# Edge stage 1 of a two-layer graph network: the gathered rows of c are added by the DMA onto a pre-activation that ACT has copied

## The chip, the cores and the metric

One Trainium2 chip, one core. The metric is the device time of one execution in microseconds (us). Lower is better. PE is TensorE, DVE is VectorE, ACT is ScalarE, POOL is GpSimd, SP is SyncE. SP and POOL issue the DMAs: SP the plain ones, POOL the indirect ones (gathers).

## The reference, cut to what matters

12,500 nodes with 128 features, 200,000 edges sorted by `dst`, 64 edge features. Layer 0 is an attention-like graph layer with a residual and a layer norm. Layer 1 is:

```python
src, dst = edge_indices[0], edge_indices[1]
edge_inputs = concatenate([x[src], x[dst], edge_features], axis=1)
h = edge_inputs @ W1 + b1
h = (h - mean(h)) * rsqrt(var(h) + 1e-5) * ln_g + ln_b
h = relu(h)
messages = (h @ W2 + b2) * sigmoid(edge_features @ gate_w + gate_b)
agg = segment_sum(messages, dst, num_segments=12500)
# then a GRU cell on (agg, x), a residual and a layer norm
```

Everything per edge up to the segment sum is edge stage 1. The part of `h` that comes from one end of the edge is made per node before the stage and is a table in HBM, `c` (12,500 rows of 128 floats). The part of the other end is a table in SBUF, `near`, one tile of 128 nodes after another. W2 is applied after the sum. W1 is centred beforehand, so the mean of `h` is zero and the layer norm needs only the sum of squares.

## The kernel before, in words

The program runs as stages one after the other: constants, a sort of the edges on DVE, a schedule, layer 0, edge stage 1 (`edge_stage1`, from line 1440), the GRU stage.

Edge stage 1 works on 1664 steps of 128 edges, in 208 groups of G = 8. Every engine has its own program over the same step numbers, made by `loop_groups`: step 0 to 207, and some steps more at the end, so that an engine can work on a group some steps after it was begun. In the text "step g" of an engine is the body of `steps(g, ...)` on that engine, and "group g-2" is the group worked on there under `has(g, 2)`. An engine's queue is in order: its step g+1 begins when its step g is issued. The engines meet by semaphores alone. R = 4 is the number of gather buffers (`crows`), edge feature buffers (`ef`) and index buffers (`cols`). The other buffers are in pairs.

One step of each engine before the change:

- SP (line 1526 on) loads the edge features, the row of node places (`spread`), and, once `hotw` and the gather of the group four before are done, the indices (`cols`) of a group.
- POOL (line 1566 on) waits for the indices and for `pre_used` of the group that had the buffer before, and issues 8 indirect DMAs (line 1559), each of 128 rows of `c` into `crows`. So it can run up to four groups ahead of DVE.
- PE, step g: turns the edge features of group g (line 1587) into `efT_ps`; makes the pre-activation `pre` of group g-1 from the turned features and from `near` by a one-hot matrix (lines 1600 and 1602), half by half; then scatters group g-3 (line 1615), for which it needs `hotw` and `z` of group g-3.
- ACT, step g: copies `efT` of group g (line 1635), makes `hotT` of group g (1641, 1645); then, when DVE has made `h` of group g-1, the exponential `eg` of the gate (1653), eight squares with their sums (1660), logarithm and exponential for the norm (`rstd`, 1666 and 1672), all of group g-1.
- DVE, step g: `h` of group g-1 = `pre` + `crows` in two halves (1703, which counts `pre_used`); then, when `rstd` of group g-2 is there, `z` of group g-2 (1712, 1728) in turns with adding the scattered sums of group g-3 (1722); `hotw` of group g-2 (1733); then the gate of group g-1 from `eg` (1743, 1745).

`h` has 129 columns: 128 for the norm, the last for the gate. `pre` fills four PSUM banks and has one buffer.

Of the kernel before, what the change touches and what calls it, by code (L numbers as in the profile page):

```python
# [20 lines left out]
ACT = mybir.ActivationFunctionType  # L21
F32 = mybir.dt.float32
# [4 lines left out]
P = 128  # L27
N = 12500
E = 200000
D = 128  # L30
# [6 lines left out]
G = 8  # L37
# [1402 lines left out]
def edge_stage1(nc, s, ins):  # L1440

    W = D + 1
    with ExitStack() as ctx:
# [14 lines left out]
        h = [sb(f"h1_{i}", [P, G, W], F32) for i in range(2)]  # L1458
# [14 lines left out]
        ef_in = [sem(f"ef_in{q}") for q in range(R)]  # L1473
        hotT_made, ef_turned, efT_made = sem("hotT1_made"), sem("ef_turned"), sem("efT_made")
        pre_made, pre_used, gate_read = sem("pre1_made"), sem("pre1_used"), sem("gate_read")
# [9 lines left out]
        with nc.Block() as block:  # L1485
# [63 lines left out]
            @block.gpsimd  # L1549
            def _(pool):  # L1550
                pool.wait_ge(zeroed, 1)
                for i in range(2):
                    nc.gpsimd.memset(z[i][:, :, D:W], 1.0).then_inc(zeroed, 1)
                for q in range(R):
                    nc.gpsimd.memset(crows[q][:, :, D:W], 0.0).then_inc(zeroed, 1)

                def gather(q):
                    for k in range(G):
                        pool.indirect_dma_start(  # L1559
                            out=crows[q][:, k, 0:D], out_offset=None, in_=s.c[:, :],  # L1560
                            in_offset=bass.IndirectOffsetOnAxis(ap=cols[q][:, 0, k:k + 1], axis=0),
                        ).then_inc(rows_in[q], 16)
                for q in range(R):
                    pool.wait_ge(cols_in[q], 16)
                    gather(q)
                with pool.Fori(1, BODIES) as o:
                    for q in range(R):
                        pool.wait_ge(cols_in[q], o * 16 + 16)

                        pool.wait_ge(pre_used, (o - 1) * (2 * R) + 2 * q + 2)  # L1570
                        pool.sem_inc(issue, 1)
                        gather(q)

            @block.tensor
            def _(pe):
                pe.wait_ge(steps_in, 32)
                pe.wait_ge(w_in, 16 * 7)
                pe.wait_ge(zeroed, R + 3)
                pe.wait_ge(added, 1)

                def steps(g, q, o):
# [9 lines left out]
                    if has(g, 1):  # L1591
# [4 lines left out]
                        for half in range(2):  # L1596
                            if used(g, 2):
                                pe.wait_ge(pre_used, g * 2 + half - 3)
# [23 lines left out]
            def _(act):  # L1622
# [4 lines left out]
                def steps(g, q, o):  # L1627
                    par, other = q % 2, 1 - q % 2
                    if has(g, 0):
                        act.wait_ge(ef_turned, g + 1)  # L1630
                        if used(g, 2):

                            act.wait_ge(pre_used, g * 2 - 2)
# [13 lines left out]
                    if has(g, 1):  # L1647
                        act.wait_ge(pre_used, g * 2)
                        if used(g, 3):
                            act.wait_ge(eg1_made, g - 2)  # L1650
                        act.sem_inc(act_go, 1)

                        nc.scalar.activation(eg[:, other, :], h[other][:, :, D], ACT.Exp,  # L1653
                                             bias=gb[:, 0:1], scale=-1.0).then_inc(gate_read, 1)
                        for half in range(2):
                            if used(g, 2) or half:
                                act.wait_ge(ss_made, g * 2 - 2 + half)
                            act.sem_inc(act_go, 1)
                            for k in range(4 * half, 4 * half + 4):
                                last = nc.scalar.activation(sq[:, k % 4, :], h[other][:, k, 0:D], ACT.Square,  # L1660
                                                            accum_out=ss[:, other, k:k + 1])
                            last.then_inc(ss_made, 1)
                        act.wait_ge(ss_made, g * 2)
# [4 lines left out]
                        act.wait_ge(ln_made, g)  # L1668
                        if used(g, 3):
                            act.wait_ge(scaled, g * 2 - 4)  # L1670
# [3 lines left out]
                loop_groups(act, steps, 1)  # L1674

            @block.vector
            def _(dve):
# [8 lines left out]
                dve.wait_ge(zeroed, R + 3)  # L1686
# [3 lines left out]
                def steps(g, q, o):  # L1690
                    par, other = q % 2, 1 - q % 2
                    if has(g, 1):
                        p1 = (q - 1) % R
                        dve.wait_ge(rows_in[p1], o * (16 * G) + (0 if q == 0 else 16 * G))
                        if used(g, 3):
# [380 lines left out]
```

## Time and profile before

| | us |
|---|---|
| median of 3 runs | 5315.48 (5291.51 to 5352.39) |
| the profiled execution's own time | 5289.88 |
| its span in the profile | 5288.0 |
| busy: PE, DVE, ACT, POOL | 3398.4, 4096.3, 2249.5, 3334.9 |

The span is what the profile sees from the first to the last instruction. Busy times are unions over the whole span, so they average over stages with different limits. Edge stage 1 is the stretch from about 2760 to 4957 us.

### The profile page before, as it was taken

How to read it: one execution, taken by the hardware profiler on the slowest of the kernel's cores; microseconds unless marked ns; L12 is line 12 of the kernel's file. 1: busy time of each engine (PE TensorE's matmuls, PEld its weight loads, DVE VectorE, ACT ScalarE, POOL GpSimd, SP SyncE). 2: the span in 40 equal slices, each digit the busy share in tenths (PEclk: the TensorE clock that was granted, in tenths of full speed). 3: DMA queues.
4: the chain of work that ended last, by engine and by line, in shares of the span. 5: the costliest groups of instructions: out<-in, count | busy, mean ns of one | idle time of the engine just before them, and what ended most of it. 6: DMA issues, size and time to landing. Idle time of an engine off the chain costs nothing. (4 is left out here: it accounts for less than half of the span.)

```text
span 5288.0 us, 106563 instructions
## 1 busy us (share of the span) xinstructions
PE 3398.4 (64%) x20476; PEld 3032.9 (57%) x20477; DVE 4096.3 (77%) x15676; ACT 2249.5 (43%) x6299; POOL 3334.9 (63%) x3474
## 2 busy tenths in 40 slices
PE   5511366666666666666647776677776776667797
PEld 4411255555555555555546765666666666667564
DVE  8998567777777777777767888888888888888655
ACT  1210123333333333333326555555555555555323
POOL 0000577777777777777757777777777777777210
PEclk9755567777777877778768889988889889998898
DMA  4100344545555555545534444444444344444102
GB/s 127 53 0 9 114 130 139 144 142 142 143 143 142 141 144 144 142 142 143 144 95 106 102 103 103 101 102 102 101 101 101 99 102 101 103 103 102 41 22 61
DMA packets 626386, 565.35 MB, mean 107 GB/s; under 512 B 376509, under 2 KB 491880, under 8 KB 625924
## 3 DMA queue, kind: packets, MB, share of 16 engines
q0 software_dynamic: 133952, 329.07, 23.0%
q1 hardware_dynamic: 492356, 235.40, 16.9%
q8 instruction: 28, 0.46, 0.0%
q14 instruction: 50, 0.41, 0.0%
HBM read 531.83 MB, written 38.57 MB: 108 GB/s over the span
## 5 line engine op out<-in xcount | busy, mean ns | idle before, releaser
L1559 POOL DMA_INDIRECT crows<-c,cols x1664 | 1659.3, 997 | 511.0 <-issue 474.9
L1115 POOL DMA_INDIRECT bxrows<-bx,cols x1664 | 1611.6, 968 | 510.0 <-issue 506.9
L1160 PE MATMUL scattered<-bxrows,hotw 128*128 128x129 f32 x3328 | 703.5, 382 | 631.3 <-DVE hotw L1321 630.8
L1160 PEld LDWEIGHTS scattered<-bxrows,hotw 128*128 128x128 f32 x3328 | 613.8, 276 | 709.8 <-DVE acc L1318 628.3
L1615 PE MATMUL scattered<-z,hotw 128*128 128x129 f32 x3328 | 585.8, 346 | 547.5 <-DVE hotw L1733 547.4
L1615 PEld LDWEIGHTS scattered<-z,hotw 128*128 128x128 f32 x3328 | 536.8, 248 | 586.3 <-issue 568.6
L1600 PE MATMUL pre<-w1e,efT 128*128 128x129 f32 x3328 | 686.5, 289 | 100.4 <-DVE h L1703 92.4
L1318 DVE TENSOR_TENSOR acc<-acc,scattered 128x129 f32 x1664 | 475.4, 286 | 326.7 <-ACT mask L1231 323.7
L1712 DVE SCALAR_TENSOR_TENSOR z<-h,rstd,ln_g 128x128 f32<-128x128 f32 x1664 | 579.5, 349 | 157.6 <-issue 157.5
L1602 PE MATMUL pre<-near,hotT 128*128 x3328 | 661.9, 282 | 0.0
L1150 PE MATMUL pre<-near,hotT 128*128 x3328 | 560.6, 338 | 147.8 <-DVE h L1297 115.8
L1150 PEld LDWEIGHTS pre<-near,hotT 128*128 128x128 f32 x3328 | 527.1, 248 | 195.9 <-issue 191.5
L1600 PEld LDWEIGHTS pre<-w1e,efT 128*128 128x128 f32 x3328 | 534.2, 202 | 134.0 <-DVE h L1703 121.1
L1321 DVE SCALAR_TENSOR_TENSOR hotw<-lane,cols,mask 128x128 f32<-128x128 f32 x1664 | 578.6, 348 | 2.3 <-ACT mask L1231 2.2
L1602 PEld LDWEIGHTS pre<-near,hotT 128*128 128x128 f32 x3328 | 528.4, 200 | 0.0
L1660 ACT ACTIVATE sq<-h 128x128 bf16<-128x128 f32 x1664 | 490.5, 296 | 25.5
L1722 DVE TENSOR_TENSOR acc<-acc,scattered 128x129 f32 x1664 | 472.5, 284 | 2.3 <-PE scattered L1615 1.0
L1224 ACT ACTIVATE sig<-logit,b 128x8 f32<-128x8 f32 x208 | 62.6, 301 | 960.5 <-DVE h L1304 960.0
L1733 DVE SCALAR_TENSOR_TENSOR hotw<-lane,cols,gate 128x128 f32<-128x128 f32 x1664 | 454.7, 347 | 0.0
L1703 DVE TENSOR_TENSOR h<-pre,crows 128x516 f32<-128x516 f32 x416 | 270.2, 691 | 199.6 <-DMA crows<-c,cols 173.3
L1653 ACT ACTIVATE eg<-h,neg_gate_b 128x8 f32<-128x8 f32 x208 | 63.9, 307 | 756.6 <-DVE h L1703 751.2
L1297 DVE TENSOR_TENSOR h<-pre,bxrows 128x512 f32<-128x512 f32 x416 | 268.2, 687 | 145.4 <-DMA bxrows<-bx,cols 135.8
(262 smaller groups left out, 5430.5 us busy)
## 6 DMA issues: line engine op xcount, KB each, us to landing
spread<-place_rows SPq DMA_DIRECT2D x416, 256.0 KB
ef<-in_edge_attr SPq DMA_DIRECT2D x1664, 32.0 KB
bxrows<-bx,cols POOLq DMA_INDIRECT x1664
crows<-c,cols POOLq DMA_INDIRECT x1664
cols<-columns SPq DMA_DIRECT2D x416, 8.0 KB, 1.9
bx<-in_x SPq DMA_DIRECT2D x1, 6250.0 KB
x_a<-in_x SPq DMA_DIRECT2D x97, 64.0 KB
x_b<-in_x SPq DMA_DIRECT2D x97, 64.0 KB
```

Of the source, the lines that this page charges most:

```text
L1115: pool.indirect_dma_start(out=bx[q][:, k, 0:2 * D], out_offset=None, in_=s.bx[:, :], in_offset=bass.IndirectOffsetOnAxis(ap=cols[q][:, 0, ...
L1150: last = nc.tensor.matmul(pre[:, k, :], hotT[par][:, k * P:(k + 1) * P], s.near[:, bass.ds(tiles[k], 1), :], start=True, stop=True)
L1160: last = nc.tensor.matmul(out[:, k // 2, k % 2, 0:W], hotw[v % 2][:, k, :], bx[v][:, k, D:D + W], start=True, stop=True)
L1318: dve.tensor_tensor(there, there, out[:, k // 2, k % 2:k % 2 + 1, 0:W], ALU.add).then_inc(added, 1)
L1321: last = dve.scalar_tensor_tensor(hotw[other][:, k, :], s.lane[:, :], cols[v].bitcast(F32)[:, 1, k:k + 1], mask[:, other, k:k + 1].to_broa ...
L1559: pool.indirect_dma_start(out=crows[q][:, k, 0:D], out_offset=None, in_=s.c[:, :], in_offset=bass.IndirectOffsetOnAxis(ap=cols[q][:, 0, k: ...
L1600: nc.tensor.matmul(pre[:, k // 2, k % 2, 0:W], efT[par][:, k // 2, :], w1e2[:, k % 2, :], start=True, stop=False)
L1602: last = nc.tensor.matmul(pre[:, k // 2, k % 2, 0:D], hotT[par][:, k * P:(k + 1) * P], s.near[:, bass.ds(tiles[k], 1), :], start=False, st ...
L1615: last = nc.tensor.matmul(out[:, bank, at:at + W], hotw[par][:, k, :], z[par][:, k, :], start=True, stop=True)
L1660: last = nc.scalar.activation(sq[:, k % 4, :], h[other][:, k, 0:D], ACT.Square, accum_out=ss[:, other, k:k + 1])
L1712: last = dve.scalar_tensor_tensor(z[par][:, k, 0:D], h[par][:, k, 0:D], rstd[:, par, k:k + 1], ln_g[:, :], ALU.mult, ALU.mult)
L1722: dve.tensor_tensor(place, place, out[:, bank:bank + 1, at:at + W], ALU.add).then_inc(added, 1)
```

## The change

ACT copies `pre` with its 129 columns from PSUM into the gather's buffer `crows`, in two halves, at its step g for group g-1. It counts them in `h_copied`. The gather of a group waits for that copy, and its DMA adds the rows of `c` onto the 128 columns that it writes (`compute_op=ALU.add`). So `crows` then holds `h`, and the addition on DVE and the buffers `h` are gone. ACT's statistics (gate exponential, squares, `rstd`) wait for the gather and move from group g-1 to group g-3 of ACT's step g. ACT's loop gets three further steps at the end in place of one. PE's next `pre` waits for `h_copied` in place of `pre_used`. DVE's parts keep their steps: `z` and `hotw` of group g-2, sums of group g-3, gate of group g-1. `z` now waits also for the scatter of group g-4. Of the edge stage nothing else changes.

```diff
-        h = [sb(f"h1_{i}", [P, G, W], F32) for i in range(2)]
@@ POOL
-                for q in range(R):
-                    nc.gpsimd.memset(crows[q][:, :, D:W], 0.0).then_inc(zeroed, 1)
                 def gather(q):
                     for k in range(G):
                         pool.indirect_dma_start(
                             out=crows[q][:, k, 0:D], out_offset=None, in_=s.c[:, :],
                             in_offset=bass.IndirectOffsetOnAxis(ap=cols[q][:, 0, k:k + 1], axis=0),
+                            compute_op=ALU.add,
                         ).then_inc(rows_in[q], 16)
                 for q in range(R):
                     pool.wait_ge(cols_in[q], 16)
+                    pool.wait_ge(h_copied, 2 * q + 2)
+                    pool.sem_inc(issue, 1)
                     gather(q)
...
-                        pool.wait_ge(pre_used, (o - 1) * (2 * R) + 2 * q + 2)
+                        pool.wait_ge(h_copied, o * (2 * R) + 2 * q + 2)
@@ PE
-                                pe.wait_ge(pre_used, g * 2 + half - 3)
+                                pe.wait_ge(h_copied, g * 2 + half - 3)
@@ ACT
-                            act.wait_ge(pre_used, g * 2 - 2)
+                            act.wait_ge(pre_made, g * 2 - 2)
...
                     if has(g, 1):
-                        act.wait_ge(pre_used, g * 2)
-                        if used(g, 3):
-                            act.wait_ge(eg1_made, g - 2)
+                        v = (q - 1) % R
+                        if used(g, 5):
+                            act.wait_ge(scaled, g * 2 - 8)
+                        for half in range(2):
+                            act.wait_ge(pre_made, g * 2 - 1 + half)
+                            act.sem_inc(act_go, 1)
+                            cut = slice(4 * half, 4 * half + 4)
+                            nc.scalar.copy(crows[v][:, cut, :],
+                                           pre.rearrange("p b t d -> p (b t) d")[:, cut, 0:W]).then_inc(h_copied, 1)
+                    if has(g, 3):
+                        v = (q - 3) % R
+                        other = (q - 3) % 2
+                        act.wait_ge(rows_in[v], (o + (0 if q < 3 else 1)) * (16 * G))
+                        if used(g, 3 + 2):
+                            act.wait_ge(eg1_made, g - 3 - 1)
                         act.sem_inc(act_go, 1)
-                        nc.scalar.activation(eg[:, other, :], h[other][:, :, D], ACT.Exp,
+                        nc.scalar.activation(eg[:, other, :], crows[v][:, :, D], ACT.Exp,
...
-                loop_groups(act, steps, 1)
+                loop_groups(act, steps, 3)
@@ DVE
-                    if has(g, 1):
-                        p1 = (q - 1) % R
-                        dve.wait_ge(rows_in[p1], o * (16 * G) + (0 if q == 0 else 16 * G))
-                        if used(g, 3):
-
-                            dve.wait_ge(scaled, g * 2 - 4)
-                            dve.wait_ge(ss_made, g * 2 - 4)
-                            dve.wait_ge(gate_read, g - 2)
-                        for half in range(2):
-                            dve.wait_ge(pre_made, g * 2 + half - 1)
-                            cut = slice(4 * half, 4 * half + 4)
-                            dve.tensor_tensor(h[other][:, cut, :],
-                                              pre.rearrange("p b t d -> p (b t) d")[:, cut, 0:W],
-                                              crows[p1][:, cut, :], ALU.add).then_inc(pre_used, 1)
...
                     if has(g, 2):
+                        v = (q - 2) % R
                         dve.wait_ge(rstd_made, g - 1)
+                        if used(g, 4):
+                            dve.wait_ge(scattered, g * 3 - 9)
                     for k in range(G):
                         if has(g, 2):
-                            last = dve.scalar_tensor_tensor(z[par][:, k, 0:D], h[par][:, k, 0:D],
+                            last = dve.scalar_tensor_tensor(z[par][:, k, 0:D], crows[v][:, k, 0:D],
```

## Rows read from the trace of the kernel before

**Rows 1.** Page, groups of POOL, DVE and ACT in the edge stage.

```profile
L1559 POOL DMA_INDIRECT crows<-c,cols x1664 | 1659.3, 997 | 511.0 <-issue 474.9
...
L1703 DVE TENSOR_TENSOR h<-pre,crows 128x516 f32<-128x516 f32 x416 | 270.2, 691 | 199.6 <-DMA crows<-c,cols 173.3
```

**Rows 2.** Stretches: start, length, busy (xcount) of PE, PEld, DVE, ACT, POOL, PEclk, DMA.

```profile
2777.00:4957.00 2180.00, 1524.18 (x10816) 1450.95 (x10816) 1816.86 (x6240) 1258.36 (x4576) 1646.08 (x1655) 0.88 0.41 100
```

**Rows 3.** Timeline of DVE, one step, 3503 to 3513 us.

```profile
3503.82 1.30 DVE L1703 TENSOR_TENSOR h<-pre,crows 128x516 f32<-128x516 f32 x2 [1.04 <-DMA crows<-c,cols]
3505.85 0.35 DVE L1712 SCALAR_TENSOR_TENSOR z<-h,rstd,ln_g 128x128 f32<-128x128 f32 x1 [0.73 <-issue]
...
3510.80 2.18 DVE L1733 SCALAR_TENSOR_TENSOR hotw<-lane,cols,gate 128x128 f32<-128x128 f32 x8
```

**Rows 4.** Timeline of ACT, 3505 to 3512.3 us.

```profile
3505.27 0.31 ACT L1653 ACTIVATE eg<-h,neg_gate_b 128x8 f32<-128x8 f32 x1 [3.88 <-DVE h L1703]
...
3508.76 0.21 ACT L1672 ACTIVATE rstd<-lnv 128x8 f32<-128x8 f32 x1 [0.20 <-ACT lnv L1666]
3509.33 0.59 ACT L1635 COPY efT<-efT_ps 128x512 f32<-128x512 f32 x1 [0.36 <-issue]
...
3511.09 1.15 ACT L1645 ACTIVATE hotT<-off,one 128x1024 f32<-128x1024 f32 x1
```

**Rows 5.** Timeline of PE at full clock, 3512 to 3519.4 us.

```profile
3512.07 2.12 PE L1615 MATMUL scattered<-z,hotw 128*128 128x129 f32 x16 [2.71 <-DVE hotw L1733]
3514.03 0.60 PE L1587 MATMUL efT_ps<-ident_f,ef 128*128 128x128 f32 x4
3515.56 0.48 PE L1600 MATMUL pre<-w1e,efT 128*128 128x129 f32 x2 [0.92 <-DVE h L1703]
...
3519.01 0.39 PE L1602 MATMUL pre<-near,hotT 128*128 x2
```

**Rows 6.** Timeline of PE, the next burst, begun at half clock.

```profile
3522.65 3.80 PE L1615 MATMUL scattered<-z,hotw 128*128 128x129 f32 x16 [3.26 <-DVE hotw L1733]
3526.25 1.06 PE L1587 MATMUL efT_ps<-ident_f,ef 128*128 128x128 f32 x4
3527.10 0.64 PE L1600 MATMUL pre<-w1e,efT 128*128 128x129 f32 x2
...
3528.38 0.39 PE L1602 MATMUL pre<-near,hotT 128*128 x2
...
3531.06 0.39 PE L1602 MATMUL pre<-near,hotT 128*128 x2
```

**Rows 7.** Stretches of 1 us around it; the fourth number is the granted clock.

```profile
3523.00:3524.00 1.00, 1.00 (x6) 0.50 0.26 72
...
3529.00:3530.00 1.00, 1.00 (x11) 1.00 0.52 120
```

**Rows 8.** Timeline of DVE, hotw of the step after that of rows 3.

```profile
3521.38 2.18 DVE L1733 SCALAR_TENSOR_TENSOR hotw<-lane,cols,gate 128x128 f32<-128x128 f32 x8
```

**Rows 9.** Timelines at the stage's start: first gather, first z, second h.

```profile
2761.03 0.95 POOL L1559 DMA_INDIRECT crows<-c,cols  x1 [1.25 <-DMA cols<-columns]
...
2791.91 0.70 DVE L1703 TENSOR_TENSOR h<-pre,crows 128x516 f32<-128x516 f32 x1 [2.03 <-PE pre L1602]
...
2796.53 1.13 DVE L1712 SCALAR_TENSOR_TENSOR z<-h,rstd,ln_g 128x128 f32<-128x128 f32 x4
```

**Rows 10.** Timelines at the stage's end: last gather, last h, last group's z.

```profile
4929.12 0.95 POOL L1559 DMA_INDIRECT crows<-c,cols  x1 [0.30 <-issue]
...
4933.95 1.30 DVE L1703 TENSOR_TENSOR h<-pre,crows 128x516 f32<-128x516 f32 x2 [2.83 <-DMA crows<-c,cols]
...
4945.02 0.35 DVE L1712 SCALAR_TENSOR_TENSOR z<-h,rstd,ln_g 128x128 f32<-128x128 f32 x1 [1.69 <-issue]
```

**Rows 11.** DMA queues from 3000 to 5000 us: packets, MB, share of 16 engines.

```profile
q0 software_dynamic: 47489, 97.35, 19.6%
```

**Rows 12.** Timeline of POOL, two gathers of one group.

```profile
3532.81 1.53 POOL L1559 DMA_INDIRECT crows<-c,cols  x1 [0.31 <-issue]
3534.65 0.95 POOL L1559 DMA_INDIRECT crows<-c,cols  x1 [0.30 <-issue]
```

More of the change, by code:

```diff
@@ L1473, in edge_stage1 @@
         ef_in = [sem(f"ef_in{q}") for q in range(R)]
+        h_copied, z_scaled_up = sem("h_copied"), sem("z_scaled_up")
         hotT_made, ef_turned, efT_made = sem("hotT1_made"), sem("ef_turned"), sem("efT_made")
-        pre_made, pre_used, gate_read = sem("pre1_made"), sem("pre1_used"), sem("gate_read")
+        pre_made, gate_read = sem("pre1_made"), sem("gate_read")
         ss_made, ln_made, rstd_made = sem("ss_made"), sem("ln_made"), sem("rstd1_made")
@@ L1577, in _ @@
                 pe.wait_ge(w_in, 16 * 7)
-                pe.wait_ge(zeroed, R + 3)
+                pe.wait_ge(zeroed, 3)
                 pe.wait_ge(added, 1)
@@ L1647, in steps @@
                     if has(g, 1):
-                        act.wait_ge(pre_used, g * 2)
-                        if used(g, 3):
-                            act.wait_ge(eg1_made, g - 2)
+                        v = (q - 1) % R
[13 more added lines that the diff above has]
+                            act.wait_ge(eg1_made, g - 3 - 1)
                         act.sem_inc(act_go, 1)
-                        nc.scalar.activation(eg[:, other, :], h[other][:, :, D], ACT.Exp,
+                        nc.scalar.activation(eg[:, other, :], crows[v][:, :, D], ACT.Exp,
                                              bias=gb[:, 0:1], scale=-1.0).then_inc(gate_read, 1)
                         for half in range(2):
-                            if used(g, 2) or half:
-                                act.wait_ge(ss_made, g * 2 - 2 + half)
+                            if used(g, 3 + 1) or half:
+                                act.wait_ge(ss_made, (g - 3) * 2 + half)
                             act.sem_inc(act_go, 1)
                             for k in range(4 * half, 4 * half + 4):
-                                last = nc.scalar.activation(sq[:, k % 4, :], h[other][:, k, 0:D], ACT.Square,
+                                last = nc.scalar.activation(sq[:, k % 4, :], crows[v][:, k, 0:D], ACT.Square,
                                                             accum_out=ss[:, other, k:k + 1])
                             last.then_inc(ss_made, 1)
-                        act.wait_ge(ss_made, g * 2)
+                        act.wait_ge(ss_made, (g - 3) * 2 + 2)
                         act.sem_inc(act_go, 1)
@@ L1667, in steps @@
                                              scale=1.0 / D).then_inc(ln_made, 1)
-                        act.wait_ge(ln_made, g)
-                        if used(g, 3):
-                            act.wait_ge(scaled, g * 2 - 4)
+                        act.wait_ge(ln_made, g - 3 + 1)
+                        if used(g, 3 + 2):
+                            act.wait_ge(scaled, (g - 3) * 2 - 2)
                         act.sem_inc(act_go, 1)
@@ L1685, in _ @@
                 dve.wait_ge(negated, 2)
-                dve.wait_ge(zeroed, R + 3)
+                dve.wait_ge(zeroed, 3)
                 spread_b = neg_b[:, :].rearrange("p (a d) -> p a d", a=1).to_broadcast([P, 4, D])
@@ L1691, in steps @@
                     par, other = q % 2, 1 - q % 2
-                    if has(g, 1):
-                        p1 = (q - 1) % R
-                        dve.wait_ge(rows_in[p1], o * (16 * G) + (0 if q == 0 else 16 * G))
-                        if used(g, 3):
-                            dve.wait_ge(scaled, g * 2 - 4)
-                            dve.wait_ge(ss_made, g * 2 - 4)
-                            dve.wait_ge(gate_read, g - 2)
-                        for half in range(2):
-                            dve.wait_ge(pre_made, g * 2 + half - 1)
-                            cut = slice(4 * half, 4 * half + 4)
-                            dve.tensor_tensor(h[other][:, cut, :],
-                                              pre.rearrange("p b t d -> p (b t) d")[:, cut, 0:W],
-                                              crows[p1][:, cut, :], ALU.add).then_inc(pre_used, 1)
                     if has(g, 3):
```

## The prediction

> **What bounds the kernel now.** I read the page's costliest groups first, then the stretch of the stage, then the timelines of the four engines over one step, since a step repeats 208 times. In the group of the gathers [rows 1] the reader is to see that POOL's busy time and its idle time, 1659.3 + 511.0, fill the stage, and that nearly all the idle time (474.9) is "issue": POOL waits for nobody. 1664 gathers from 2761.03 to 4930.07 [rows 9, 10] are 1.30 us each, 10.4 us for the 8 of a group. DVE's addition in the same rows shows the other side: it stood 173.3 us waiting for the gather's data, 0.83 us per group. DVE was busy 1816.86 of 2180 us, ACT 1258.36 and PE 1524.18 [rows 2], so each has room in a period of 10.4 us. The stage goes at POOL's pace. From the first z at 2796.53 to that of the last group at 4945.02 [rows 9, 10] there are 207 periods, 2148.5 / 207 = 10.38 us each.
>
> **What the order of the steps allows.** Before, the statistics of a group are made one ACT step earlier than the z that needs them asks for: ACT makes rstd of group g-1 in its step g, DVE uses it in its step g+1. That slack lets ACT, DVE and PE work side by side. The change moves ACT's statistics back by two groups (to g-3 in step g) and leaves z at group g-2 of DVE's step g. So DVE's step g now needs ACT's step g+1, a step ahead of it. Follow what ACT's step g+1 needs before it reaches the statistics of group g-2:
>
> - PE's turn of the features of group g+1, and both halves of `pre` of group g, for the new copies. These are PE's step g+1.
> - PE's step g+1 is queued behind its step g, whose last part is the scatter of group g-3. It waits for `hotw` of group g-3, which DVE makes near the end of its step g-1.
>
> So a ring closes over one step: end of hotw in DVE's step g-1, scatter, turn, pre (PE), copy and statistics (ACT), z to hotw in DVE's step g. Nothing in it overlaps with anything else in it, apart from what is counted below. The gate (1743, 1745) needs `eg` of ACT's step g+2 at the end of DVE's step g, which lies on the same ring, 3.4 us before rstd, and costs nothing more. The length of this ring is the period, if it is above 10.4 us.
>
> **The ring's length, step by step.**
>
> - DVE from z to the end of hotw: 3505.85 to 3510.80 + 2.18 = 3512.98, 7.13 us [rows 3].
> - PE begins the scatter 0.91 us before that end, as the first half of hotw is enough: 3512.07 against 3512.98 [rows 3, 5], and likewise 3522.65 against 3521.38 + 2.18 = 3523.56 [rows 6, 8].
> - PE's burst scatter, turn, pre. The clock decides here. At full clock the scatter begins at 3512.07, the turn ends at 3514.63, and pre takes 3515.56 to 3519.40, 3.84 us [rows 5]. In [rows 5] pre still waited for DVE's h. After the change it follows the turn at once (its wait is for a copy one period old), begins at 14.5 and ends at 18.4. In [rows 6] the burst begins after 3.26 us of idle time at the half clock (0.50, 1.2 GHz), and is unbroken: scatter 3.80, turn until 3527.31, pre from 3527.10, the spacing falls from 0.43 to 0.22 us at 3528.38, the end is 3531.45. [Rows 7] show the granted clock at 0.50 in 3523 to 3524 and 1.00 from 3529.
> - ACT: the turned features are copied 0.15 us after the turn ends (that is the lag between DVE's h ending at 3505.12 and eg starting at 3505.27 [rows 3, 4]). From the efT copy to the end of hotT it is 3509.33 to 3512.24, 2.91 us. Then the copies of pre. The trace has no copy of 128x516 out of PSUM on ACT. The nearest is efT, 128x512 PSUM to SBUF, 0.59 us [rows 4]. I take 0.59 for each half. It can't be much below, and twice that, 1.2 us, is my upper bound (DVE's add of the same shape, with a second input, takes 0.69 [rows 1]); at that bound the ring is 0.6 us longer, +125 us in all, inside the range. The second half counts after pre ends: lag 0.15 + 0.59.
> - Statistics, from eg to the end of rstd: 3505.27 to 3508.97, 3.70 us [rows 4]. Then 0.15 us to z. The 0.73 us "issue" ahead of z in [rows 3] is register loading of tile numbers, and now lies beside the ring, between gate and rstd.
>
> With the full clock throughout, from z at 3505.85: pre ends 3518.40, second copy 3519.14, rstd 3522.84, z 3522.99. ACT's own path is shorter (14.63 + 0.15 + 2.91 = 17.69, then the first copy until 18.28). Ring 17.1 us.
>
> With the burst as in [rows 6]: hotw ends 3523.56, pre ends 3531.45, second copy 3532.19, rstd 3535.89, z 3536.04: 12.48 us after hotw's end, plus 7.13 = 19.6 us. With the half clock throughout the spacing would stay at 0.43 after 3528.38: 12 spacings by 0.21 and a longer last matmul, 2.8 us later [rows 6]. Ring 22.4 us.
>
> After the change PE is idle between pre and the next scatter for 19.6 - 8.8 = 10.8 us, three times the 3.26 us after which it began at the half clock in [rows 6]. So every burst begins slow. Its length unbroken is that of [rows 6], so I take it as it stands: 19.5 us, a little below 19.6 as ACT's second copy may begin without the full lag.
>
> **What lies beside the ring.** DVE loses the addition, 1.30 us per group [rows 3]. Before, it ran while POOL set the pace, and after, it isn't on the ring: it gives nothing. ACT gains 1.2 us per group: counted. POOL issues the same 8 DMAs, 10.4 us per group. It now starts a group when both copies of it are made, and ACT needs the data two ACT steps later, about 39 us minus the statistics. So 10.4 us of issue and 3.9 us of landing (last gather 4930.07 to last h 4933.95 [rows 10]) are covered with a margin of more than 20 us, and POOL's pace hides under 19.5 us as long as a gather takes less than 19.5 / 8 = 2.4 us against 1.30. SP's queue: indices of a group wait for hotw and gather of the group four before, and the features of the next group stand behind them. That wait ends with DVE's step g-2, a whole period before PE's step g+1 needs the features; before it was the same, with a shorter period. The memsets of crows on POOL and the third and fourth waits (`scaled`, `scattered`) are for things long done: nothing.
>
> **The gather with an addition** isn't in the trace. From below, its issue costs what the plain one costs, 0.95 us and 0.30 us between two [rows 12]; nothing that it leaves out would make it cheaper. From above I have only far rows: the longest plain one in the step of [rows 12] took 1.53 us, in place of the 0.95 of its neighbour. The transfer: 47489 packets took 19.6% of 16 engines over 2000 us [rows 11], 0.13 us each, 32 packets to one gather of 1484, 2 for each DMA engine. Reading the destination as well makes this perhaps 0.5 to 0.8 us for each engine per gather, against 2.4 us. I take it as hidden. If it isn't, the stage follows it (a rival below).
>
> The Trainium skill's page "DMA: Bandwidth & Descriptors", section "Rules for kernel authors", says that an accumulating DMA reads its destination and writes it later. That speaks against the change: each row is read twice and written once. It gives no price, no row here shows one, and by my bound it stays below the ring.
>
> **The sum.** The first z now needs the first gather, which before ran beside everything from 2761. Second half of pre at 2791.9 [rows 9], copy until 2792.5, 8 gathers at 1.25 [rows 12] = 10.0 us, landing 3.9, statistics 3.7, z at about 2810.2: 13.7 us later than 2796.5. Then 207 periods of 19.5 us = 4036.5 in place of 2148.5: +1888. The last two rings have no turn and no pre, about 6 us less each: -12. Together +1890. 5288.0 + 1890 = 7178 span, and with the 1.9 us around it 7180 us. The profiled execution (5289.88) lies 0.5% below the median of the runs, 5315.48, and inside their range. A measurement of this kernel tells about 1% from no change; this is 36%.
>
> **Rivals.**
>
> 1. *The clock takes another course, ring as said.* Full clock always (17.1 us): 5290 + 207 x 6.7 + 2 = 6680. Half clock always (22.4): 7780. For the first speaks nothing, with 10 us of idle time; for the second that the trace has few bursts after so long a gap. These are the bounds of my own case.
> 2. *The gather with an addition becomes the bound.* At 3.0 us each, 24 us per group: 5290 + 207 x 13.6 + 2 = 8110, and growing with its price, from 2.4 us on. For it: POOL is the bound now, and the operation is unknown. Against: it would have to cost nearly twice the plain one.
> 3. *Not slower.* The ring doesn't bind, because PE's pre of group g runs beside or ahead of the scatter's wait for hotw, and POOL stays the bound. It decides below 10.4 us of ring. Then DVE's shed 1.30 us gives nothing, but POOL's gathers could fall to 0.95 + 0.30 = 1.25 us each (8 x 1.25 = 10.0): 5290 - 207 x 0.38 + 14 = 5225. Against it: every engine takes its queue in order, and in [rows 5] the scatter stood 2.71 us waiting for hotw with the turn of the next group behind it.
> 4. *The addition doesn't run as one DMA* but in pieces with their own waits, so that the landing passes 39 us and holds up ACT. It ends slower too, above 8100. A part of case 2 for the numbers.
>
> **How the numbers follow.** Ring as forecast, with its clock bounds: 0.81 (own range 6680 to 7780). Gather-bound, cases 2 and 4: 0.13. Not slower: 0.04, half of it within 1% and half faster by over 1%. Slower by some other, smaller amount (a shorter ring of 11 to 16 us because I missed an overlap): 0.02. The range 6680 to 7800 leaves out the gather-bound case, the not slower one, and a little at each end. Chances: faster by over 1% 0.02; within 1% 0.02; slower by over 1% 0.81 + 0.13 + 0.02 = 0.96.
>
> **What the profile after would show.** If right: z (DVE) starts every 19 to 20 us; between the gate and z DVE stands 7 to 8 us waiting, put down to ACT's rstd or eg; ACT waits for pre of PE ahead of its copies; PE stands some 10 us ahead of the scatter waiting for hotw, and its granted clock over the stage falls from 0.88 to 0.6 to 0.8; POOL, idle about 9 us per group, waits for ACT's copy. Wrong, if POOL's gathers stand back to back (case 2 with a longer mean, case 3 with the old one), if ACT's wait ahead of eg is for the DMA, or if the period is below 16 us.

## The result and the profile after

The changed kernel took 7034.48 us (median of 4 runs, 7020.41 to 7085.32), the kernel before beside it 5303.49 us. Ratio 1.326, 95% interval 1.3145 to 1.3374. The profiled execution has a span of 7019.3 us against 5288.0, 1731 us more.

Five of the page's costliest groups after. Columns: line, engine, operation, tiles, shapes and count; busy us, mean ns of one; idle us of the engine just before them, and what ended most of it.

```profile
L1557 POOL DMA_INDIRECT crows<-c,cols x1664 | 2722.0, 1636 | 1191.0 <-ACT crows L1656 745.9
...
L1616 PE MATMUL scattered<-z,hotw 128*128 128x129 f32 x3328 | 757.4, 418 | 2213.5 <-DVE hotw L1735 2213.5
...
L1745 DVE TENSOR_SCALAR eg<-eg 128x8 f32<-128x8 f32 x208 | 35.7, 172 | 1719.3 <-ACT eg L1666 1719.3
L1714 DVE SCALAR_TENSOR_TENSOR z<-crows,rstd,ln_g 128x128 f32<-128x128 f32 x1664 | 574.4, 345 | 629.6 <-ACT rstd L1685 627.6
L1636 ACT COPY efT<-efT_ps 128x512 f32<-128x512 f32 x208 | 121.9, 586 | 2235.8 <-PE efT_ps L1588 2235.8
```

Read these as a circle. ACT stands 2235.8 us waiting for PE's turn (line 1588, the edge features turned into `efT_ps`), PE 2213.5 for DVE's hotw, DVE 1719.3 + 627.6 for ACT's eg and rstd. Each waits some 11 us in each of 208 steps for the engine before it, and none is the bound by its own work. POOL, which before waited for hardly anyone (36.1 of its 511.0 us idle weren't issue), waits 745.9 us for ACT's copies. So the gathers aren't the bound either, although one now takes 1.64 us in place of 1.00.

The stretch of the stage after, columns as in [rows 2]:

```profile
2900.00:6600.00 3700.00, 1588.31 (x10244) 1540.29 (x10244) 1476.19 (x5516) 1379.68 (x4728) 2580.72 (x1577) 0.68 0.36 56
```

PE is busy 43% of it, DVE 40%, ACT 37%. Before it was 70, 83 and 58% [rows 2]. The granted clock's mean fell from 0.88 to 0.68.

The period is best read from one line: the first and the last start of DVE's hotw, between which lie 207 periods and 1.9 us inside a group. For line 1735 the view of one source line (duration in ns min/median/max, first and last start) has:

```profile
L1735 DVE SCALAR_TENSOR_TENSOR hotw<-lane,cols,gate x1664: 336/343/371, 2812.6 to 6683.3; 128x128 f32<-128x128 f32 x185
```

and the same line of the kernel before:

```profile
L1733 DVE SCALAR_TENSOR_TENSOR hotw<-lane,cols,gate x1664: 337/348/384, 2800.1 to 4952.2; 128x128 f32<-128x128 f32 x185
```

(3870.7 - 1.9) / 207 = 18.69 us per group against (2152.1 - 1.9) / 207 = 10.39. The first hotw came 12.5 us later. 12.5 + (3870.7 - 2152.1) = 1731.1 us, the whole difference of the spans. Nothing is left over for another stage.

18.69 is a mean over all periods, and the last two are shorter. From DVE's timeline (start, length):

```profile
6662.76 2.18 DVE L1735 SCALAR_TENSOR_TENSOR hotw<-lane,cols,gate 128x128 f32<-128x128 f32 x8
...
6672.27 2.18 DVE L1735 SCALAR_TENSOR_TENSOR hotw<-lane,cols,gate 128x128 f32<-128x128 f32 x8
...
6681.51 2.18 DVE L1735 SCALAR_TENSOR_TENSOR hotw<-lane,cols,gate 128x128 f32<-128x128 f32 x8
```

They take 9.5 and 9.2 us. The 205 ahead of them, from 2812.61 to 6662.76, are 18.78 us each.

One turn of the ring after, in the order in which the work goes. DVE's timeline:

```profile
4805.23 2.18 DVE L1735 SCALAR_TENSOR_TENSOR hotw<-lane,cols,gate 128x128 f32<-128x128 f32 x8
4814.97 0.17 DVE L1745 TENSOR_SCALAR eg<-eg 128x8 f32<-128x8 f32 x1 [7.56 <-ACT eg L1666]
...
4818.38 0.35 DVE L1714 SCALAR_TENSOR_TENSOR z<-crows,rstd,ln_g 128x128 f32<-128x128 f32 x1 [3.00 <-ACT rstd L1685]
...
4823.32 2.18 DVE L1735 SCALAR_TENSOR_TENSOR hotw<-lane,cols,gate 128x128 f32<-128x128 f32 x8
```

PE's timeline, two bursts:

```profile
4806.50 3.40 PE L1616 MATMUL scattered<-z,hotw 128*128 128x129 f32 x16 [10.73 <-DVE hotw L1735]
4809.74 0.60 PE L1588 MATMUL efT_ps<-ident_f,ef 128*128 128x128 f32 x4
...
4813.55 0.39 PE L1603 MATMUL pre<-near,hotT 128*128 x2
4824.59 3.80 PE L1616 MATMUL scattered<-z,hotw 128*128 128x129 f32 x16 [10.66 <-DVE hotw L1735]
4828.18 1.06 PE L1588 MATMUL efT_ps<-ident_f,ef 128*128 128x128 f32 x4
...
4832.77 0.39 PE L1603 MATMUL pre<-near,hotT 128*128 x2
```

ACT's timeline, the first turn and the copies of the second:

```profile
4810.54 0.59 ACT L1636 COPY efT<-efT_ps 128x512 f32<-128x512 f32 x1 [10.38 <-PE efT_ps L1588]
...
4812.30 1.15 ACT L1646 ACTIVATE hotT<-off,one 128x1024 f32<-128x1024 f32 x1
4813.35 1.29 ACT L1656 COPY crows<-pre 128x516 f32<-128x516 f32 x2
4814.54 0.31 ACT L1666 ACTIVATE eg<-crows,neg_gate_b 128x8 f32<-128x8 f32 x1
...
4818.03 0.21 ACT L1685 ACTIVATE rstd<-lnv 128x8 f32<-128x8 f32 x1 [0.20 <-ACT lnv L1679]
...
4832.26 0.57 ACT L1656 COPY crows<-pre 128x516 f32<-128x516 f32 x1
4833.28 0.59 ACT L1656 COPY crows<-pre 128x516 f32<-128x516 f32 x1 [0.46 <-PE pre L1603]
```

hotw ends at 4807.41. PE has begun 0.91 us earlier, turns until 4810.34, ends pre at 4813.94. ACT takes the turned features 0.20 us after, copies pre until 4814.64, has rstd at 4818.24, and z starts at 4818.38. hotw ends at 4825.50, 18.1 us after the last. That is the first of the two rings shown. In the second PE's burst (scatter, turn and pre, one after the other) takes 8.57 us in place of 7.44, since its clock rises later. Stretches of 1 us, columns as in [rows 2], the granted clock third from the end:

```profile
4809.00:4810.00 1.00, 1.00 (x10) 1.00 (x9) 0.00 (x0) 0.00 (x0) 0.86 (x1) 0.83 0.45 56
...
4828.00:4829.00 1.00, 1.00 (x6) 1.00 (x6) 0.00 (x0) 0.00 (x0) 0.78 (x1) 0.50 0.20 22
4829.00:4830.00 1.00, 1.00 (x8) 1.00 (x7) 0.00 (x0) 0.56 (x2) 0.92 (x1) 0.59 0.56 71
```

The first burst began at 4806.50, and in the stretch from 4809 its clock is at 0.83; the second began at 4824.59 and is still at 0.50 from 4828 and at 0.59 from 4829. The second ring is 19.2 us. In both, and in every one of the 205, ACT's second copy begins 0.12 us after pre ends: it is PE's burst that ACT waits for there.

The mean of each part over the 205 rings adds up to the period: burst 8.09, less the 0.91 that lie before hotw's end; 0.12 to the second copy; 0.49 from it to eg; statistics 3.71; 0.17 to z; z to the end of hotw 7.11. Together 18.78.

POOL's timeline in the same turn:

```profile
4810.99 1.55 POOL L1557 DMA_INDIRECT crows<-c,cols  x1 [0.30 <-issue]
4815.43 1.55 POOL L1557 DMA_INDIRECT crows<-c,cols  x1 [2.89 <-ACT crows L1656]
```

The last gather of a group ends at 4812.54, POOL waits for the copy and goes on at 4815.43, 2.89 us later. Per group its slack is 18.7 less 8 x 1.94, 3.2 us in the mean.

### The profile page after: what moved, and what is told of

It is laid out like the page before. It is cut to its first block and busy times, and to the rows that moved or that the text cites. A ratio compares the mean times of both kernels' runs of the same rounds, so it can differ in the third digit from the quotient of the medians.

```text
span 7019.3 us, 107281 instructions
## 1 busy us (share of the span) xinstructions
PE 3555.0 (51%) x20476; PEld 3209.9 (46%) x20477; DVE 3837.5 (55%) x15260; ACT 2448.3 (35%) x6715; POOL 4396.3 (63%) x3470
## 3 DMA queue, kind: packets, MB, share of 16 engines
q0 software_dynamic: 320320, 329.07, 24.2%
## 5 line engine op out<-in xcount | busy, mean ns | idle before, releaser
L1557 POOL DMA_INDIRECT crows<-c,cols x1664 | 2722.0, 1636 | 1191.0 <-ACT crows L1656 745.9
L1616 PE MATMUL scattered<-z,hotw 128*128 128x129 f32 x3328 | 757.4, 418 | 2213.5 <-DVE hotw L1735 2213.5
L1616 PEld LDWEIGHTS scattered<-z,hotw 128*128 128x128 f32 x3328 | 707.5, 323 | 2252.2 <-issue 2219.8
L1745 DVE TENSOR_SCALAR eg<-eg 128x8 f32<-128x8 f32 x208 | 35.7, 172 | 1719.3 <-ACT eg L1666 1719.3
L1714 DVE SCALAR_TENSOR_TENSOR z<-crows,rstd,ln_g 128x128 f32<-128x128 f32 x1664 | 574.4, 345 | 629.6 <-ACT rstd L1685 627.6
L1636 ACT COPY efT<-efT_ps 128x512 f32<-128x512 f32 x208 | 121.9, 586 | 2235.8 <-PE efT_ps L1588 2235.8
L1673 ACT ACTIVATE sq<-crows 128x128 bf16<-128x128 f32 x1664 | 490.2, 297 | 25.5
L1304 DVE SCALAR_TENSOR_TENSOR h<-h,w 128x128 f32<-128x128 f32 x1664 | 369.1, 285 | 0.0
```

The costliest lines, as they stand in the source:

```text
L1557: pool.indirect_dma_start(out=crows[q][:, k, 0:D], out_offset=None, in_=s.c[:, :], in_offset=bass.IndirectOffsetOnAxis(ap=cols[q][:, 0, k: ...
L1616: last = nc.tensor.matmul(out[:, bank, at:at + W], hotw[par][:, k, :], z[par][:, k, :], start=True, stop=True)
L1673: last = nc.scalar.activation(sq[:, k % 4, :], crows[v][:, k, 0:D], ACT.Square, accum_out=ss[:, other, k:k + 1])
L1714: last = dve.scalar_tensor_tensor(z[par][:, k, 0:D], crows[v][:, k, 0:D], rstd[:, par, k:k + 1], ln_g[:, :], ALU.mult, ALU.mult)
```

## The experiments

They ran on four chips. On three of them (experiments 1 to 4, 5 to 8, 9 to 11) the kernel before took 6864, 6883 and 6899 us in place of 5303, and layer 0, which nobody edited, was longer too. On the fourth (experiment 12) it took 5308. So a total is compared only with totals of the same chip, and I read the period of the edge stage from the line of hotw. For the changed kernel that is sound: its period there (experiment 8) is the same to the last digit. For another kernel it is sound where the trace shows that the engine that bounds it isn't SP, and I say where it is.

**1. Statistics first.** In ACT's step the statistics of group g-3 are moved ahead of the rest:

```diff
 def steps(g, q, o):            # ACT
+    if has(g, 3):
+        ...                    # wait for the gather, eg, squares, lnv, rstd
     if has(g, 0):
         ...                    # efT, off, hotT
     if has(g, 1):
         ...                    # the two copies of pre into crows
-    if has(g, 3):
-        ...
```

> Edit to the changed kernel: in ACT's step g the statistics of group g-3 come first, ahead of the efT, hotT and the copies of pre. Nothing else changes. Theory A (the ring DVE hotw, PE scatter, turn and pre, ACT copies and statistics, DVE z closes over one step and sets the period of 18.7 us): the ring now closes over two steps, 19 to 20 us for two, so about 10 us each, and the next bound is POOL's issue of the gathers with addition, 8 x (1.64 + 0.30) = 15.5 us per group. Period 15.5 us, about 3.2 x 207 = 660 us less than the changed kernel's 7034: about 6370. Theory B (gather's transfer and the waits of POOL for the copies set the period): no change, about 7030. If POOL were no bound even then: 5250.

Measured: 6857.22 us, 0.9991 (0.9946 to 1.0037) of the kernel before on that chip. The line of hotw, and POOL's timeline:

```profile
L1735 DVE SCALAR_TENSOR_TENSOR hotw<-lane,cols,gate x1664: 335/340/354, 3350.6 to 6505.4; 128x128 f32<-128x128 f32 x185
```

```profile
4999.23 1.55 POOL L1557 DMA_INDIRECT crows<-c,cols  x1 [0.30 <-issue]
5001.09 1.55 POOL L1557 DMA_INDIRECT crows<-c,cols  x1 [0.30 <-issue]
...
5010.91 1.55 POOL L1557 DMA_INDIRECT crows<-c,cols  x1 [0.30 <-issue]
```

The period is 15.23 us, forecast 15.5. The total forecast, 6370, didn't allow for this chip; against the changed kernel there (7650 in experiment 8, 7618 in experiment 2, on two chips of that kind) it is 793 and 761 us less. 3.46 x 207 = 716 of them are the period. The rest lies outside it: between the profiled executions the first hotw comes 69 and 25 us earlier, and 25 and 11 us less follow the last. POOL's gathers stand back to back: the ring is open, and the next bound is the gather. No work was taken away, only an order changed.

**2. Plain gather** (the addition left out: crows holds the rows of c alone).

```diff
-                            compute_op=ALU.add,
```

> Edit to the changed kernel: the gather is a plain one, without the addition; what is left out is the sum, so that crows holds the rows of c alone. All waits and the order of the steps stay. Theory A (the ring sets the period, POOL isn't on it): POOL's gathers fall to about 1.0 us each and POOL's wait for the copies grows by as much, the period stays at 18.7 us, about 7030 in all, within 1%. Theory B (the dearer gather, 0.64 us more for each of 1664, is on the path): 1060 us less, about 5970.

```profile
L1734 DVE SCALAR_TENSOR_TENSOR hotw<-lane,cols,gate x1664: 339/345/352, 3375.8 to 7246.4; 128x128 f32<-128x128 f32 x185
```

3870.6 us between the two, the changed kernel has 3870.7. The gathers fell to 994 ns each, some 1067 us of POOL's work went, and the period didn't move by 0.01 us. (The whole took 7618.31 us on that chip; the 7030 of the forecast was for the first one.) The time went into POOL's wait, as a row of this kernel's page shows:

```profile
L1557 POOL DMA_INDIRECT crows<-c,cols x1664 | 1654.5, 994 | 2261.8 <-ACT crows L1655 1777.9
```

**3. Both** (the addition left out). 

> Both edits: statistics first in ACT's step, and the plain gather (the sum is left out). Theory A: the ring is open and POOL is back at 10.4 us per group, so the time is that of the kernel before plus the later first z (about 14 us): about 5310. If the open ring is longer than 10.4 us per step, up to 5600. Theory B (order of the steps is nothing, the gather is all): the same as the plain gather alone.

Measured 6550.94 us, 0.9516 (0.9404 to 0.9628) of the kernel before there; period (2834.3 - 1.9) / 207 = 13.68. Less than with either edit alone, so theory B falls, but not 10.4, and the 5310 to 5600 us of theory A were missed. The bound is SP. PE's waits for SP's loads of the features (from the view of line 1517, who waited for it: us, times):

```profile
  PE efT_ps L1587: 461.8, 204
```

and all that SP itself waited for in the stretch 3800 to 4900 us, here and in experiment 1 (us, times, longest):

```profile
SPq L1530 <- PE efT_ps L1587: 0.4, 2, 0.3
```

```profile
SPq L1538 <- DVE hotw L1735: 536.1, 72, 7.9
```

SP hardly waits for anyone: the eight issues of a group take a median of 10.1 us, where they take 4.0 in the kernel before on the first chip. Experiments 5 and 12 follow this up.

**4. Half of the squares** (the norm of four of eight steps left out; their sums are a constant).

```diff
-                            for k in range(4 * half, 4 * half + 4):
+                            for k in range(4 * half, 4 * half + 2):
...
+                dve.memset(ss[:, :, :], 128.0)
```

> Edit to the changed kernel: ACT makes 4 of the 8 squares of a group; the sums of the other four columns are a constant, so that their norm is left out. This takes 4 x 0.293 = 1.17 us out of a term that by theory A is on the ring: period 18.7 to 17.5 us, 208 x 1.17 = 243 us less, about 6790. Theory B (gather sets the period): no change, about 7030, and POOL's wait for ACT's copies would stay.

```profile
L1736 DVE SCALAR_TENSOR_TENSOR hotw<-lane,cols,gate x1664: 334/341/356, 3347.8 to 7038.6; 128x128 f32<-128x128 f32 x185
```

Period (3690.8 - 1.9) / 207 = 17.82 us, 0.87 us less than the changed kernel, and 7395.48 us in all. Against experiment 2 on the same chip, which has the changed kernel's period, hotw from first to last is 180 us shorter, forecast 243. So the squares lie on the ring. The statistics fell by 1.19 us, from 3.71 to 2.52, and 0.3 of them came back, as the traces' means show: 0.11 in PE's burst (8.20 in place of 8.09), whose clock rises at another point, and 0.19 between rstd and z (0.35 in place of 0.17). Why z starts later behind a shorter wait, no run tells.

**5. The kernel before, again.** 

> The kernel before, unchanged, for a profile on the chip of this job. On the chip of the first four experiments the kernel before took 6864 us in place of 5303, and layer 0, which no edit touches, was some 520 us longer there. Expected on a chip like the first one: hotw from first to last start in the edge stage 2152 us, 10.4 us per group. On a chip like that of the first four experiments: 15 us per group, and the profile should name the engine that is late (I expect SP, whose DMA issues are uneven there).

6912.08 us, period (3187.3 - 1.9) / 207 = 15.39. Its POOL, and the issues of the features on SP (line 1517), against the latter in the kernel before on the first chip:

```profile
L1559 POOL DMA_INDIRECT crows<-c,cols x1664 | 1656.5, 996 | 1560.1 <-DMA cols<-columns 955.7
```

```profile
L1517 SPq FUSED_REGOPS  x1664: 2/46/2097, 3368.9 to 6554.7; - x185
```

```profile
L1517 SPq FUSED_REGOPS  x1664: 46/46/51, 2771.3 to 4905.9; - x185
```

A register instruction of 46 ns (duration in ns min/median/max), never over 51 on the first chip, takes up to 2097 ns here. The eight issues of a group last 9.5 us in the median and up to 22.4, against 4.0 and at most 5.4 there. One group of each, from SP's timeline:

```profile
5017.99 11.66 SPq L1517 DMA_DIRECT2D ef<-in_edge_attr  x8
```

```profile
4007.23 4.01 SPq L1517 DMA_DIRECT2D ef<-in_edge_attr  x8
```

POOL then waits for indices that SP loads late. So SP is late on these chips, and that is shown; why SP stumbles on these chips, no run tells.

**6. The kernel before with the gather that adds** (the sum is another one: crows grows).

```diff
-                    nc.gpsimd.memset(crows[q][:, :, D:W], 0.0).then_inc(zeroed, 1)
+                    nc.gpsimd.memset(crows[q][:, :, :], 0.0).then_inc(zeroed, 1)
...
                             in_offset=bass.IndirectOffsetOnAxis(ap=cols[q][:, 0, k:k + 1], axis=0),
+                            compute_op=ALU.add,
...
+                pool.wait_ge(zeroed, R + 3)
```

> Edit to the kernel before: the gather adds onto crows (which is cleared once and then keeps growing, so the sum is another one), DVE's addition and the order of the steps stay. This measures the dearer gather by itself, where there is no ring. Theory A: POOL, the bound before, goes at 8 x (1.60 to 1.64 + 0.30) = 15.2 to 15.5 us per group in place of 10.4, so the edge stage is 4.9 x 207 = 1010 us longer than the kernel before on a quiet chip, 6320 us, still shorter than the changed kernel by 700 us. Theory B (the gather's price shows only together with the wait for the copies): no change against the kernel before.

```profile
L1559 POOL DMA_INDIRECT crows<-c,cols x1664 | 2607.9, 1567 | 507.5 <-issue 481.3
```

Idle almost only by "issue" (481.3 of 507.5): POOL is the bound. (3095.6 - 1.9) / 207 = 14.95 us per group, near 8 x (1.567 + 0.305) = 14.98. So the dearer gather by itself would have cost about 4.6 us per group on the first chip, 944 us (an estimate: this period less the 10.39 of the first chip); the ring above it another 3.74 us, 774 us. On this chip the total, 6790.40 us, can't be told from the kernel before (0.9862, 0.9721 to 1.0003), whose period there is 15.39, with POOL waiting for SP's indices (experiment 5). The total of 6320 was forecast for a quiet chip and wasn't tried on one.

**7. Both, again.** 

> Statistics first in ACT's step and the plain gather (the sum is left out), once more. Theory A on a quiet chip: 10.4 us per group, about 5310 us, within 1% of the kernel before. On a chip where SP is late: the same period as the kernel before has there or less.

6570.27 us, period 13.66, as in experiment 3 and below the 15.39 of the kernel before on the same chip. PE waits for the features as in experiment 3 (452.8 us, 201 times).

**8. The changed kernel, again.** 

> The changed kernel, unchanged, for its time on the chip of this job. Theory A: 18.7 us per group whatever the chip's SP does, as the ring leaves SP 7 us and more of slack: hotw from first to last start 3870 us. In all 7034 on a quiet chip, about 7600 on one like that of the first four experiments, where the plain gather took 7618.

```profile
L1735 DVE SCALAR_TENSOR_TENSOR hotw<-lane,cols,gate x1664: 337/343/348, 3419.7 to 7290.4; 128x128 f32<-128x128 f32 x185
```

7650.52 us, and 3870.7 us between the two, as on the first chip. The 607 us by which the first hotw comes later (3419.7 against 2812.6) are the stages before. Its ratio to the kernel before is 1.1111 here (1.0953 to 1.1270) and 1.326 on the first chip: the ring hides what SP does, the kernel before doesn't.

**9. Half the width** (on experiment 1; half of the addition left out, other rows).

```diff
-    out=crows[q][:, k, 0:D], out_offset=None, in_=s.c[:, :],
+    out=crows[q][:, k, 0:D // 2], out_offset=None, in_=s.c.rearrange("n (a d) -> (n a) d", a=2),
```

> Edit to the kernel with statistics first: the gather adds rows of 64 floats (256 B) onto the first half of each row of crows, in place of 128 floats (512 B); half of the addition is left out and the rows read are others. There the gather's issue on POOL sets the period, so the mean of one gather is read from the period. If the dearer issue (1.60 against 1.00 us) is paid per row or per packet: 1.6 us and 15.2 us per group as before. If per byte: about 1.3 us or less, and 12.8 us per group.

```profile
L1557 POOL DMA_INDIRECT crows<-c,cols x1664 | 2653.1, 1594 | 540.7 <-issue 505.1
```

1594 ns against 1597 with the full width (experiment 1). One row then holds 256 bytes in place of 512, so the price isn't per byte. The time, 6860.35 us, is that of one execution and says no more. Over the changed kernel's whole run the gathers' queue moved 320320 packets, against 133952 before, with the same 329.07 MB. The difference, 186368, is 1664 x 112: a plain gather is 32 packets, one that adds 144, as many as one for each of the 128 rows and 16 more. Whether POOL pays for the packets or for a second read, this doesn't tell.

**10. Both, a third time.** 

> Statistics first and plain gather, for the third time, hoping for a chip on which the kernel before takes 5300 us. There theory A expects 10.4 us per group and 5310 us, within 1% of the kernel before; a rival (the open ring itself is longer, 13.6 us as on the chips where SP's issues are uneven) expects 5970. On a chip of the other kind nothing new: 13.6 us.

6537.71 us, the third chip of the other kind, period 13.69, with PE waiting for the features again (451.1 us, 200 times): nothing new.

**11. Statistics first, again.** 

> Statistics first with the gather that adds, again. 15.2 us per group whatever the chip. In all 6310 where the kernel before takes 5300 (1.19 times), and 0.99 to 1.00 times the kernel before where that takes 6870.

6851.67 us, 0.9970 (0.9909 to 1.0031) of the kernel before; period 15.22. As forecast.

**12. Both, with half of the feature loads** (experiment 3's kernel; besides the addition, half of the loads from the fifth group on are left out).

```diff
-                def load_features(g, q, features):
+                def load_features(g, q, features, loads=G):
...
-                    for k in range(G):
+                    for k in range(loads):
...
-                            load_features(o * R + q, q, features)
+                            load_features(o * R + q, q, features, G // 2)
...
-                        pe.wait_ge(ef_in[q], o * (16 * G) + 16 * G)
+                        pe.wait_ge(ef_in[q], o * (16 * G // 2) + 16 * G)
```

> Edit to the kernel with statistics first and plain gather: from the fifth group on, SP loads the edge features of 4 of the 8 steps of a group; the other half keeps the features of the first four groups, so half of the loads are left out. Theory (on these chips the open ring's 13.7 us per group is SP, which takes 8 to 11 us to issue 8 loads in place of 4.0, and the open ring itself is not above POOL's 10.4 us): the period falls to 10.4 us, POOL's gathers stand back to back at 1.0 + 0.3 us, hotw from first to last start is about 2150 us, and the time is 680 us less than the 6538 of the third run. Rival (the open ring is 13.7 us long by itself): no change, 6538.

```profile
L1557 POOL DMA_INDIRECT crows<-c,cols x1664 | 1695.1, 1019 | 603.7 <-issue 503.7
```

This came on a fourth chip, where the kernel before took 5308.38 us and SP's register instructions stay at 46 to 51 ns, so it doesn't test SP; that SP bounds experiment 3 is shown by the waits there. It does refute the rival that the open ring is 13.7 us long. Period (2260.5 - 1.9) / 207 = 10.91 us (forecast 10.4), POOL nearly back to back. That is the slower of the two executions: 5492 and 5388 us lie too far apart for a ratio, and both lie above the kernel before's. So with the order mended, and even with an addition that costs nobody anything, no run shows an edge stage below the 10.39 us per group of the kernel before. That fits POOL as the bound before: what DVE was relieved of wasn't.

## Why the prediction was right

The forecast was 7180 us, range 6680 to 7800, slower with 0.96. Measured 7034.

**The bound before and the ring.** Right. Experiments 1, 2 and 4 separate it from the gather: opening the order takes 3.46 us out of the period, making the gather cheap takes out nothing, and taking 1.19 us out of ACT's statistics takes out 0.87.

**Its length.** 19.5 us forecast, 18.78 measured over the first 205 rings; this is the term that was mis-sized, 0.72 x 205 = 147 us of the 1890. The terms one by one, as means over these rings: DVE from z to hotw 7.13, measured 7.11. Start of the scatter 0.91 ahead, the same. Copy of a half 0.59, measured 0.59. Statistics 3.70, measured 3.71. From rstd to z 0.15, measured 0.17. From the end of pre to eg 0.74, measured 0.61: 0.12 to the second copy, and eg begins 0.10 before that copy ends. What was off most is PE's burst. I took one burst of [rows 6], 8.8 us, for every one. After, the mean is 8.09 us, and two neighbours take 7.44 and 8.57, by where in the burst the clock rises: ahead of the turn in one (0.60 us, full speed) and in `pre` in the other (the turn takes 1.06). ACT's own path (efT, off, hotT, first copy) never holds up the second copy, as forecast, but in the shortest bursts it ends within 0.01 us of pre. That each burst begins at the half clock was right: the 16 matmuls of the scatter take at least 3.39 us in all 208 bursts, where at the full clock they take 2.12 [rows 5]. The stretch's mean of 0.68 lies in the forecast 0.6 to 0.8.

**The gather with an addition.** I took its issue as near that of the plain one and hidden. Hidden is right, the price wasn't: 1.64 in place of 1.00 us, 15.5 us per group. It left a slack of 3.2 us, not 9. The prediction's own threshold was 2.4 us with the gap between two, and 1.94 is nearer to it than to 1.30. For rival 2 it takes only 0.4 us more. The upper bound by far rows, 1.53 us, was passed in the mean. That the forecast held all the same, it owes to the ring's length and not to the price that it gave. The transfer was sized well: 0.5 to 0.8 us for each DMA engine per gather, and measured 0.55 (from 3000 to 5000 us the gathers' queue took 23.3% of 16 engines for 122832 packets, 853 gathers).

The rule of the page "DMA: Bandwidth & Descriptors" (the Trainium skill, "Rules for kernel authors"), that an accumulating DMA reads its destination and writes it later, has no price. The traces give what the whole operation costs: POOL is held 1.56 to 1.64 us for 128 rows, and the queue has 144 packets in place of 32. That it is the reading of the destination that costs, no run shows.

**First z and the tail.** Forecast 13.7 us later, and 12 less for the last two rings. The first z and hotw came 12.5 later. The last two rings take 9.5 and 9.2 us, together 18.8 less than two of 18.78. The forecast had taken off only turn and pre; ACT's copies fall away as well, DVE's gate waits for nothing there, and z only 2.0 and 1.8 us, so that little more is left than z to hotw (7.1). With the 147 us of the ring, the 8 of these two, 1.2 of the first z and 1.7 between counting from z to z and from hotw to hotw, that is the 158 us by which the forecast 1890 lies above 1731.

**What was said of the profile after.** DVE's wait was put at 7 to 8 us per group, between the gate and z. It is 3.0 there, and 8.3 more ahead of the gate, 11.3 in all. The sentence counted one of two waits and had it in the wrong place. The ring's length less DVE's work, 19.5 - 7.1, would have given 12.4. POOL's idle time was put at 9 us per group; with the dearer gather it is 5.7 (1191.0 / 208). The rings take 18.0 to 19.8 us, where z was to start every 19 to 20. Of ACT's waits nearly all is ahead of the copy of the turned features, and only 81.0 us ahead of the copies of pre, where the forecast had it.

**Rival 3, not slower.** Its mechanism, PE's pre running ahead of the scatter's wait, is seen nowhere: in both timelines of PE the turn follows the scatter. It took an opened ring, a plain gather and half of the feature loads to come near the kernel before's pace on the fourth chip (experiment 12); the first two alone were run only on chips where SP is late.

## What to carry to other kernels

When a value is handed over in one step's order, write down for each engine which group it works on in its step, before and after. If a consumer moves closer to its producer than the steps in between allow, the engines run one after the other, and the period becomes the sum of one chain that can be worked out from a trace of before. Taking work from an engine that isn't the bound gives nothing, and giving it to the one that is costs, here some 4.6 us per group even without the ring (experiment 6). When the expected gain doesn't come, move one block in an engine's queue before changing what the block does.

## What was not expected of the hardware

- A gather that adds onto SBUF holds POOL 1.56 to 1.64 us for 128 rows (means of the runs), a plain one 0.99 to 1.02, and the price is the same for rows of 256 and of 512 bytes (1594 and 1597 ns).
- It goes out as 144 packets in place of 32, at the same number of bytes.
- PE's burst of 52 matmuls, begun at the half clock after some 10.7 us of idle time, took 7.3 to 9.0 us, by where in it the clock rose.
- The same program took 5303 us on the first chip, 5308 on that of experiment 12 and 6864 to 6899 on three others. There SP's small instructions took now and then up to 2.1 us in place of 0.05 (experiment 5), and SP became the bound of a kernel whose POOL was quick enough (experiment 3). The changed kernel, whose 18.7 us leave SP slack, kept its period to 0.01 us on both kinds of chip, and statistics first has 15.2 us on two of the three; the kernel before went from 10.39 to 15.39. A verdict between two orders can so depend on the chip: with the statistics first the changed kernel equals the kernel before there, while on a chip like the first one its period, 15.2 against 10.4, would put it near 6300 us (an estimate: 5288 + 12.5 + 4.84 x 207).
